# One core, four layers: the order of all parts and the table of PSUM banks replaced, and a wait added in front of the reciprocals of the heads' sums

## The reference

```
xn = layernorm(x)
layer 0: causal attention, 16 heads of 16, learned biases      + SiLU gate/up FFN of 1024 units with
                                                                 ternary weights (groups of 64) and an RMS norm
layer 1: gated recurrence: causal conv, L2-normed q and k,     + mixture of 16 experts (top 2, capacity 128)
         scan over time, two group norms, output gate            and one shared expert
layer 2: attention of one head of 256                          + SiLU FFN of 1024 units whose weights are
                                                                 cubic splines of control points
layer 3: attention, 16 heads of 16, rotary embedding           + mixture of 8 experts (top 2, dense) and one shared expert
```

## Time and profile before

| | |
|---|---|
| median of the three runs | 1364.27 us |
| the profiled execution | 1363.54 us |
| its span, first to last instruction | 1362.2 us |
| around the span | 1.3 us |
| mean granted clock of TensorE | 0.945 of full speed |

### The profile page before, as it was taken

How to read it: one execution, slowest core, us unless ns; L and a number is a source line. 1 busy time by engine, 2 the same in 40 slices (tenths; PEclk the granted TensorE clock), 3 DMA queues, 4 the chain that set the end, 5 groups by cost and what they waited for, 6 DMA issues and landing times.

```text
span 1362.2 us, 19768 instructions
## 1 busy us (share of the span) xinstructions
PE 1214.3 (89%) x7753; PEld 796.7 (58%) x7772; DVE 975.4 (72%) x1840; ACT 658.8 (48%) x961; POOL 423.3 (31%) x402
## 2 busy tenths in 40 slices
PE   1789999999999776699689999999899899989998
PEld 0568777677655333355337888888446445545544
DVE  8977466776758998986378663548976878767671
ACT  4345565765665464445113241321484385276373
POOL 5455540034003140531444330235213323321320
PEclk9879999999999788899858999999799899999999
DMA  6200000002140000016412300001500100100110
GB/s 179 97 1 1 1 1 2 2 1 72 45 131 32 0 32 0 32 62 217 151 50 42 34 22 1 0 1 24 120 1 1 47 1 2 47 0 1 49 45 16
DMA packets 31436, 53.24 MB, mean 39 GB/s; under 512 B 4880, under 2 KB 19440, under 8 KB 30576
## 3 DMA queue, kind: packets, MB, share of 16 engines
q1 hardware_dynamic: 27264, 41.02, 9.5%
q0 software_dynamic: 4080, 10.97, 3.6%
HBM read 44.03 MB, written 10.52 MB: 40 GB/s over the span
## 4 chain that ended last, share of the span: by engine, by line
PE 61%; DVE 21%; issue 7%; ACT 6%; POOL 3%; DMA 2%; DVEq 0%; POOLq 0%; ACTq 0%
PE pair L646 20%; PE bank L646 16%; PE bank L734 6%; PE pair L702 5%; PE pair L722 4%; DVE max L1142 3%; PE pair L684 3%; ACT probs L1649 2%; PE pair L692 1%; PE pair L713 1%; DMA gathered<-outbox,slots 1%; POOL gathered L2004 1%; DVE xn L1061 1%; PE bank L742 1%; PE pair L915 1%
## 5 line engine op out<-in xcount | busy, mean ns | idle before, releaser
L1142 DVE TENSOR_REDUCE max<-pair 128x2 f32<-128x1024 f32 (+3 forms) x256 | 254.5, 1020 | 95.9 <-PE pair L692 51.5
L1649 ACT ACTIVATE probs<-pair 128x1024 f32<-128x1024 f32 (+3 forms) x256 | 212.7, 867 | 93.0 <-PE pair L692 53.6
L702 PE MATMUL pair<-ks,qs 50*128 50x512 f32 (+3 forms) x512 | 113.6, 460 | 17.9 <-DVE max L1142 5.9
L1962 POOL TENSOR_TENSOR h_low<-hidden,h_high 128x512 fp32r<-128x512 f32 x64 | 83.1, 1303 | 147.1 <-ACT h_high L1684 146.9
L734 PE MATMUL bank<-probs,v 128*32 128x512 f32 (+3 forms) x1024 | 114.0, 524 | 1.6 <-ACT probs L1649 1.4
L722 PE MATMUL pair<-qs,ks 52*128 52x512 f32 (+3 forms) x512 | 106.5, 435 | 5.9 <-ACT qs L1637 2.2
L2022 POOL TENSOR_TENSOR h<-mix_h,h 128x512 bf16<-128x512 f32 x48 | 55.7, 1172 | 133.2 <-DVE mix_h L1546 71.2
L702 PEld LDWEIGHTS pair<-ks,qs 50*128 50x128 f32 x512 | 49.7, 194 | 74.7 <-DVE max L1142 28.3
L722 PEld LDWEIGHTS pair<-qs,ks 52*128 52x128 f32 x512 | 47.4, 185 | 75.2 <-issue 19.6
L1676 ACT ACTIVATE hidden<-pair 128x512 f32<-128x512 f32 x64 | 37.6, 597 | 93.7 <-PE pair L646 78.0
L1192 DVE SCALAR_TENSOR_TENSOR hidden<-hidden,pair 128x512 f32<-128x512 f32 x64 | 43.6, 681 | 44.0 <-ACT hidden L1676 43.8
(11 more groups left out here) (334 smaller groups left out, 2993.6 us busy)
## 6 DMA issues: line engine op xcount, KB each, us to landing
expert_in<-in_experts_in SPq DMA_DIRECT2D x16, 352.0 KB, 4.7
expert_out<-in_experts_out SPq DMA_DIRECT2D x16, 256.0 KB, 5.7
h<-comb SPq DMA_DIRECT2D x4, 1024.0 KB, 5.1
tern_raw<-in_ffn_in SPq DMA_DIRECT2D x8, 256.0 KB, 3.6
x<-in_x SPq DMA_DIRECT2D x4, 512.0 KB, 5.7
inbox<-zeros SPq DMA_DIRECT2D x4, 512.0 KB, 6.3
tokens<-inbox SPq DMA_DIRECT2D x16, 128.0 KB, 3.1
outbox<-expert_y SPq DMA_DIRECT2D x16, 128.0 KB, 3.1
```

The lines of the kernel that those rows point to most:

```text
L702: made = mm(to[:, hh, 0:n], m.qs[g % 2][r0:r0 + AUG + 2, p, qt * P:(qt + 1) * P], m.ks[g % 2][r0:r0 + AUG + 2, p, 0:n], start=True, stop=k ...
L1142: V.tensor_reduce(m.max[:, g % 2, qt, 2 * p:2 * p + 2], to[:, :, 0:n], AX.X, ALU.max).then_inc(*s.done("top"))
L1649: A.activation(m.probs[(2 * kt + p) % 4][:, :, q0:T], to[:, :, q0:T], ACT.Exp, scale=0.25).then_inc(*s.done("exp"))
L1962: Q.tensor_tensor(m.h_low[k][:, j, :], m.hidden[k][j % 2][:, :], m.h_high[k][:, j, :].bitcast(F32), ALU.subtract).then_inc(*s.done("low"))
```

## The change

Of the lists in `DUE` and `TAKEN`, 163 are replaced. No part is added or taken away, and no instruction's shape changes. 310 of 1190 PE parts, 503 of 1022 on DVE, 256 of 853 on ACT, 121 of 283 on POOL and 66 of 98 on SP have another place on their engine; most go one to three places, the furthest 29. The one new operation is a wait in `headed`: the reciprocal waits for the `headed` that used the same half of `inv_sum`, two groups back. It is issued 28 times.

```diff
 DUE = { ...
-    "gate": "474 473 475 476 494 491 499 495 512 507 508 504 526 527 536 533",
...
-    "count": "480 500 520 535",
...
-    "spline": "612 613 614 617 615 618 619 620 621 624 626 625",
...
-    "route_root": "318 346 362 398",
...
+    "gate": "474 473 478 476 495 492 498 494 513 505 509 503 526 528 536 533",
...
+    "count": "481 501 521 534",
...
+    "spline": "613 612 614 615 617 616 619 620 618 624 628 626",
...
+    "route_root": "318 347 364 401",
...
-    "spline": "240420402042",
+    "spline": "042420024400",
...
@@ -1155,6 +1155,9 @@
         dve.wait_ge(*at("back", k, b, g))
         if b > 0:
             dve.wait_ge(*at("rows", k, b - 1))
+        if 4 * b + g >= 2:
+            b2, g2 = (b, g - 2) if g >= 2 else (b - 1, g + 2)
+            dve.wait_ge(*at("headed", k, b2, g2))
         V.reciprocal(inv, cols[:, :, D]).then_inc(*dve.up())
```

More of the change, by code:

```diff
@@ L314 @@
 TAKEN = {name: [int(bank) for bank in banks] for name, banks in {
-    "tern_sum": "024022442024",
-    "turn": "0040004240020004",
-    "qkv": "00402022240402444204400200422424",
-    "fold": "2020424204420402040442242442000200244040222004222004240242242440",
-    "score": "4224440242220402022444002044200242004042404440224440000024040442220440004420220440040424204244204024042240004404020044420042224024040042422002402442220022004402402000200402444042242004404220244422444240224004242440040224222024440002440244200204242402022442",
@@ L320 @@
-    "refold": "42220222220004224000400220442042",
-    "prob": "4400402024042440204222400044042240200240222424240240200202422424240404204422202404422002404022024242222440424042024404402004400444020442000442402404204204222204224242044200004242042020440420420240024242020240404040000220420242200042422002042400040402044202",
-    "weigh": "66667777666677777777666677776666777777776666777766667777666666667777666677776666777766667777666677776666777766667777666677776666",
-    "back": "77766766666767676776777676766676",
@@ L324 @@
-    "rows": "202424402204",
-    "out": "67667776676777767677767776767676",
-    "unit": "0224404020440420200404204002400240200442024240240424020420400224",
-    "down": "76676677",
-    "mean": "6766",
-    "proj": "4204244022422224",
-    "gate": "6767776666677667",
-    "gamma": "2024",
-    "inflow_turn": "4420",
-    "mem_turn": "76777676",
-    "shared": "2040204242242400",
+    "tern_sum": "024004004202",
+    "turn": "2444402002040404",
+    "qkv": "42242022024242222402022424002020",
+    "fold": "0202422424404240404202422402222440202042004024222020042042200242",
@@ new lines @@
+    "score": "2002424020000420044424002222000040224240240422042224444442424220004024440204224000000202424400440420442202420020242200040204240204440220224020440420002202044402440224444040244442042024040424204442424240040422040442242004200420040424204002242044040420400420",
+    "refold": "42402002022040422024420220400440",
+    "prob": "4400402024044220402444442244240002024024000202024024040042020202024240240000404220020202040422420204444002040204242004040202200224040242444240424204200204222400004040244020004202404202422442040240204040202042424242422442040222044420200220240224242402244020",
@@ new lines @@
+    "weigh": "66667777666677777777666677776666777777776666777766667777666666667777666677776666777766667777666677776666777766667777666677776666",
+    "back": "77766767666767676777767676766676",
+    "rows": "044420024404",
+    "out": "67667776676776767677767776767676",
+    "unit": "0404424220440420200202400442244042402004420240240440422002200442",
+    "down": "77676677",
+    "mean": "6766",
+    "proj": "2404244244224002",
+    "gate": "6767777676777666",
+    "gamma": "2000",
+    "inflow_turn": "4202",
@@ L335 @@
+    "mem_turn": "76767776",
+    "shared": "4024420424022444",
     "count": "6667",
     "merge": "76",
-    "expert_turn": "7676777777667667",
-    "expert_in": "4020044240240442",
-    "expert_fold": "6667676776677666",
+    "expert_turn": "7677777777767667",
+    "expert_in": "0242400224024002",
+    "expert_fold": "6667676766677666",
     "expert_out": "6667766767767766",
-    "spline": "240420402042",
+    "spline": "042420024400",
     "qk2": "2024",
-    "v2": "76767676",
-    "score2": "6766667667666676",
@@ L345 @@
-    "probs_turn": "7767767667777676",
+    "v2": "76766666",
+    "score2": "6766667667766676",
+    "probs_turn": "7766767667777676",
     "comb_turn": "6767",
-    "mix": "202024224424444224400204244000022200044020240244",
+    "mix": "404042000420000024022024244000022200242404024022",
 }.items()}
```

## The result

The changed kernel took 1377.23 us (median of 5 runs, 1371.24 to 1378.12), the kernel before 1364.27. The ratio is 1.0088, 95% interval 1.0068 to 1.0107: 12 us slower by the ratio (13 by the medians), outside the range of 1356 to 1370. On a second chip it was 1.0100 (1.0083 to 1.0117).

The account below looks back on a forecast made before the run. PE, busy 89% of the span, was taken as the bound, with DVE bounding the start-up and layer 1. Terms 0.03 + 0 + 1.7 - 3.2 = -1.5 us on 1363.54, plus 0.7 to the median, gave 1362.8 us; range 1356 to 1370.

Parts of the forecast that it names:

- the one on layer 3 and the start-up: Start-up, layer 0 and most of layer 3: reordering costs 0, bounds plus and minus 3 us.
- four combines: Start of layer 2, DVE: three combines moved earlier free up to 2.8 us of DVE; PE sees 2.14.
- Layer 1: Layer 1: router delay +5.1 us less 3.4 us of DVE waits gone, +1.7 us; bounds -3.4 and +5.1.
- that sign: Layer 1: right if the root before route_d3 ends 3 us or more behind DVE's arrival.
- the 1.45 us that `gate31` was to add: Layer 1, PE: gate31 between rows11 and the outs adds 1.98 us, less 0.53 us of absorbed wait.
- Layer 2: Layer 2: later splines at the start outweighed by waits and lost clock that go, -3.2 us; bounds 0 and -6.4.
- the -1.2 forecast: Start of layer 2: unit201 starts 1.2 us earlier, with two splines of 2.2 us each left behind it.
- The added wait: DVE's reciprocals in the attention: 0.03 us each, only the last one counts, +0.03 us; bounds 0 and 7.3.
- C: Rival, chance 0.22: layer 1's delay comes in full, its gain and layer 2's do not; 1369.4 us.
- D: Rival, chance 0.08: holes between splines keep PE's clock low past the start of layer 2; 1367 us.
- B: Rival, chance 0.20: route_d3 is not delayed, layer 1 keeps its 3.4 us and layer 2 gains 3.2; 1357.7 us.
- new bank waits of over 3 us: Layer 3 or layer 0: such waits would show the prediction wrong.

Follow-up runs that it names:

- based_moved: Kernel before plus the added wait, with POOL's based30 and based32 of layer 3 moved behind the first rope_cos of their batch: ratio 1.0013 (1.0002 to 1.0024).
- only_s1: Kernel before plus the added wait, with only layer 1 and the experts in the changed orders and banks: ratio 0.9986 (0.9966 to 1.0006).

## Why the prediction was wrong

**The step that failed** is the one on layer 3 and the start-up: "Parts change places by one to three, none is added, and the bounding engine has the same work ... I take 0. Bounds: plus and minus 3 us." The runs showed +2.3 us for the start-up and layer 0, and +6.6 for layer 3. DVE had the same instructions, but they took 6.0 us longer in layer 3: products of 0.41 us took up to 2.6 beside POOL's work. Of the 93 parts of POOL's order there, 41 changed place, and the prediction went through none; POOL's order alone cost 3.4 us and gave 6 back. It made DVE's products slow and put `set_pool3` late. How much of the cost is either stays open. PE's lower clock came on top, and of the start-up's 2.3 us the cause was not looked for.

**The rule was in hand.** The prediction quoted the Trainium skill, "SBUF — State Buffer", section "Who interferes with whom", for four combines, and showed it in the earlier trace rows. It said that by the rule "the sum would not change, since moved combines only meet other POOL work". It asked this of one place; the question belonged to each POOL part that moves against DVE. `rope_b` at 0.41 us, beside a POOL instruction of 2.38 us, is the case that the rule describes, and based_moved agrees with it. At the combines themselves the gain came as the rows had it: `combine11` took 0.97 us and `combine10` with `combine13` 1.89, where `combine11` and `combine10` had taken 4.83.

**Layer 1: the order of events right, the delay mis-sized.** ACT, changed kernel:

```profile
580.40 1.28 ACT L1779 ACT_TABLE_LOAD   x1 [3.46 <-PE bank L646]
581.69 0.59 ACT L1779 ACTIVATE shared_h<-pair 48x512 f32<-48x512 f32 x1
582.30 1.28 ACT L1796 ACT_TABLE_LOAD   x1
583.59 0.26 ACT L1796 ACTIVATE route_log<-route_u 128x64 f32<-128x64 f32 x1
```

The root stands behind the tanh, as forecast, and ends at 583.85 in a trace that came into layer 1 some 2.6 us later than that of the kernel before. On the scale of the prediction that is 581.2, where 587.1 - 3.4 = 583.7 was forecast. `route_d3` starts 0.03 us behind it:

```profile
583.88 0.23 DVE L1371 TENSOR_TENSOR route_u<-route_log,route_bias 128x64 f32<-128x64 f32 x1 [0.93 <-ACT route_log L1796]
...
593.23 0.17 DVE L1422 CAST slots<-route_position 128x8 int32<-128x8 f32 x1
```

`route_e3` ends 0.9 us later than in the earlier trace rows, so 1.7 us earlier on that scale. DVE waited 0.93 us for the root (0.94 in only_s1), where the prediction had 5.4 and called 3 or more a sign of being right: that sign failed. Two sizes were off. PE, changed kernel, `rows11` and the end of the last `out`:

```profile
563.59 1.09 PE L754 MATMUL pair<-ident_r,normed 128*128 128x128 f32 x8 [2.12 <-DVE normed L1322]
...
579.10 1.22 PE L646 MATMUL bank<-shared_w,shared_h 128*128 128x256 f32 x4
```

From the start of `rows11` to the end of the last `out` PE took 16.7 us, for 16.9 before: the 1.45 us that `gate31` was to add did not appear, and `rows11` started 4.4 us earlier on the scale of before, not 3.4. And DVE was done with the two `joined` and reached `route_d3` at 582.95, 1.4 us earlier than before on that scale and not 3.4. The wait in front of `flow2` is gone. So layer 1 lost nothing: the forecast was +1.7, only_s1 measured -2 (+0.8 to -4.6 by its interval). For PE the prediction took 7 us, the upper end of its "5.4 to 7", which no row gives. No drain shows behind the loads, as before the change: 581.68 to 581.69.

**Layer 2: one gain right, two losses not seen.** `v201` waits no more, as forecast; `weight203` was done at 765.6 as forecast, but `probs_turn03` waited 1.16 us all the same, now for `v2_out11` (L1488), since `v211` has moved ahead of it on PE and its copy stands behind the combine that waits for gathered3:

```profile
778.52 0.66 PE L958 MATMUL bank<-ident_r,probs 128*128 128x128 f32 x4 [1.16 <-DVE v L1488]
```

Against the gain `turn20` waited 2.84 us for `norm203`, which now stands behind combine12, `cubic3` and `spline_sum20`:

```profile
710.54 1.94 PE L665 MATMUL pair<-ident_r,xn 128*128 128x128 f32 x8 [2.84 <-DVE xn L1061]
```

And `unit201` started no earlier (718.0, with 2.8 us of lag) for the -1.2 forecast. The end of layer 2, 2.6 us, was in no term: the prediction listed the three stats, not the norms, and did not ask what stood behind them.

**The added wait** was right at nothing; DVE 1266.85 + 0.26 to 1267.14, the same 0.03 us as in the earlier trace rows:

```profile
1266.85 0.26 DVE L1161 RECIPROCAL inv_sum<-bank 128x16 f32<-128x16 f32 x1 [1.47 <-PE bank L742]
1267.14 0.42 DVE L1163 TENSOR_TENSOR heads<-bank,inv_sum 128x256 f32<-128x256 f32 x1
```

**The rivals.** The loss came, but by none of them. C placed it in layer 1, D in the clock at the start of layer 2. The clock did fall, but in layer 3. B was the nearest to layer 1, which its time had at -3.4 us: `route_d3` waited 0.93 us only. It had the whole at 1357.7 all the same, since it too put layer 3 at nothing. Of the signs, "new bank waits of over 3 us" in layer 3 did not appear: the loss is made of shorter ones, 2.17 us at most, of slower products and of the clock.

## What to carry to other kernels

When an order is changed, go through the engines that are not the bound as well: for each instruction of POOL that moves, ask which DVE instruction it now runs beside, and price that one by a row where the two meet. Ask too whether the POOL instruction is still done before its reader, for the same move can make POOL itself late. A search that takes each part's duration as fixed can't see this. And look for waits in chains of three queues: the part that PE waits for may be late because ACT's queue holds it for a DVE part that stands behind work nobody is waiting for.

## What was not expected of the hardware

A DVE TENSOR_TENSOR of two SBUF inputs, 128x256 f32, took 0.41 us alone and 2.44 to 2.60 us beside a 128x1024 TENSOR_TENSOR of POOL that had begun before it, and ended 0.3 us behind it; POOL's `based32` took 2.38 us with and without. A norm (TENSOR_SCALAR, 128x256) also grew, from 0.4 to 1.42 us, beside POOL. A wait of 1.76 us on PE was followed by the lower clock, and eight products took 1.91 us for 1.07. Executions of kernels with the same layer 3 differ by 6 us in that layer alone, and most of those of the kernel before lay between 1359 and 1369 us, so only the rounds told effects under 0.3% from nothing.
